# An attention-and-FFN kernel on one Trainium2 core: part of the sync engine's transfers re-ordered at the start of the FFN stage and at each change of token group

## The reference

```python
h  = einsum('bct,bcd->bdt', x, cond_weights[itok])       # a 64x64 mix per sequence
x  = x + attention(h)      # 16 heads of 32, 8 key/value heads, rope, the best 32 of 64 keys per head
hx = x @ W.T + scalings[a] * ((x @ A[a].T) @ Bm[a].T)    # a linear layer with a rank-16 adapter per sequence
Wg, Wu, Wd = dequant_nvfp4(...)                          # 4096x512, 4096x512, 512x4096, four-bit codes with scales
inter = gelu(hx @ Wg.T) * (hx @ Wu.T)
out   = x + inter @ Wd.T
```

## Time and profile before

| | before |
|---|---|
| median of 3 runs | 2748.27 us (2748.01 to 2749.01) |
| the profiled execution | 2745.64 us, of which the span from first to last instruction is 2744.1 us |
| PE busy | 2588.6 us, 94% of the span |
| PEld, DVE busy | 2171.9 us (79%), 1964.2 us (72%) |
| ACT, POOL busy | 881.2 us (32%), 977.2 us (36%) |
| mean granted TensorE clock | 0.984 of full |
| SP's queue of transfers | 481.17 MB, 48.1% of the 16 engines' time |
| from 753 to 1950 us | transfers busy 78%, 290 GB/s; POOL busy 623.88 us |
| from 1950 us to the end | transfers busy 53%, 198 GB/s; POOL busy 28.30 us |

### The profile page before, as it was taken

The page is one execution under the profiler, slowest core; times in us unless marked ns, Lnnn a source line. Parts: engine busy times, 40 slices in busy tenths (PEclk is TensorE's granted clock), DMA queues, the critical chain, the costliest instruction groups (busy, mean ns, idle before and its releaser), DMA issues.

```text
span 2744.1 us, 38773 instructions
## 1 busy us (share of the span) xinstructions
PE 2588.6 (94%) x13824; PEld 2171.9 (79%) x13824; DVE 1964.2 (72%) x3084; ACT 881.2 (32%) x1530; POOL 977.2 (36%) x1189
## 2 busy tenths in 40 slices
PE   5888999898889989999999999999999999999999
PEld 4777888787768778788887778887888888888887
DVE  6887777878569778788887788888854554545555
ACT  4445445454322222222222222222222222222222
POOL 3554434534246445555554455555410000000000
PEclk9999999999999999999999999999999999999999
DMA  3223222322679888758887866678645744664363
GB/s 119 84 94 105 81 96 93 105 87 86 242 293 326 334 314 319 280 216 327 306 325 279 329 246 240 223 288 306 237 167 216 272 154 165 226 261 158 146 250 138
DMA packets 173617, 585.34 MB, mean 213 GB/s; under 512 B 22136, under 2 KB 81400, under 8 KB 139008
## 3 DMA queue, kind: packets, MB, share of 16 engines
q1 hardware_dynamic: 138112, 481.17, 48.1%
q0 software_dynamic: 35328, 101.82, 10.0%
HBM read 446.14 MB, written 136.71 MB: 212 GB/s over the span
## 4 chain that ended last, share of the span: by engine, by line
PE 75%; DMA 11%; DVE 8%; issue 2%; ACT 2%; SPq 1%; POOL 0%; DVEq 0%; ACTq 0%; POOLq 0%
PE bank_a L866 22%; PE down L883 21%; PE proj L693 11%; PE bank_b L866 11%; DMA out<-acc 7%; PE bank_c L866 6%; DMA gu_slot<-w_scratch 4%; PE scores L733 1%; PE pv L758 1%; PE scores L742 1%; DVE probs L1259 1%; DVE hs L1193 1%; DVE rope_sin L1213 1%; DVE row_sum L1252 1%; DVE rope_in L1215 1%
## 5 line engine op out<-in xcount | busy, mean ns | idle before, releaser
L883 PE MATMUL down<-d_slot,inter_parts 128*128 128x512 f32 x3072 | 737.4, 389 | 0.0
L883 PEld LDWEIGHTS down<-d_slot,inter_parts 128*128 128x128 f32 x3072 | 576.6, 188 | 119.7
L1092 ACT ACTIVATE copy_p<-bank_a 128x512 f32<-128x512 f32 x384 | 229.7, 598 | 798.0 <-PE bank_a L866 798.0
L866 PE MATMUL bank_a<-h_ahead,gu_slot 128*128 128x512 f32 x1536 | 402.8, 399 | 46.8 <-DMA gu_slot<-w_scratch 43.4
L1401 DVE TENSOR_TENSOR acc<-down,acc 128x512 f32<-128x512 f32 x512 | 349.6, 686 | 88.4 <-PE down L883 60.7
L866 PE MATMUL bank_a<-h_once,gu_slot 128*128 128x512 f32 x1536 | 390.0, 389 | 1.4 <-ACT copy_p L1092 1.4
L866 PEld LDWEIGHTS bank_a<-h_ahead,gu_slot 128*128 128x128 f32 x1536 | 295.1, 193 | 113.3 <-DMA gu_slot<-w_scratch 47.6
L866 PEld LDWEIGHTS bank_a<-h_once,gu_slot 128*128 128x128 f32 x1536 | 288.2, 188 | 61.9 <-ACT copy_p L1092 2.2
L574 POOL TENSOR_TENSOR lut_v<-lut_v,signed_scale 128x512 f32<-128x512 f32 x96 | 124.4, 1296 | 495.0 <-DVE lut_v L1182 494.3
L1386 DVE TENSOR_TENSOR up<-gate,up 128x512 f32<-128x512 f32 x256 | 214.0, 836 | 87.7 <-ACT gate L1102 73.9
L1109 ACT ACTIVATE inter_parts<-up 128x512 fp32r<-128x512 f32 x256 | 159.4, 629 | 271.0 <-PE down L883 158.8
(11 more groups left out here) (123 smaller groups left out, 3536.1 us busy)
## 6 DMA issues: line engine op xcount, KB each, us to landing
gu_slot<-w_scratch SPq DMA_DIRECT2D x128, 1792.0 KB, 8.5
d_slot<-d_scratch SPq DMA_DIRECT2D x64, 1024.0 KB, 10.4
w_scratch<-w_parts POOLq DMA_DIRECT2D x96, 512.0 KB, 7.7
h_ahead<-h_scratch SPq DMA_DIRECT2D x44, 1024.0 KB, 11.7
h_once<-h_scratch SPq DMA_DIRECT2D x33, 1024.0 KB, 7.6
h_scratch<-h_out SPq DMA_DIRECT2D x32, 896.0 KB, 5.0
acc<-out SPq DMA_DIRECT2D x22, 1024.0 KB, 5.9
out<-acc SPq DMA_DIRECT2D x22, 1024.0 KB, 13.6
```

The costliest lines, as they stand in the source:

```text
L866: ins = pe.matmul(bank[:], gu_slot[n % 2][:, w, u, c * P:(c + 1) * P], mat(v, h)[:, c, part, :], start=(start and c == 0 and i == 0), stop ...
L883: ins = pe.matmul(bank[:], inter_parts[:, j, u, q, e * P:(e + 1) * P], d_slot[m % 2][:, j, part, :], start=(j == 0 and i == 0), stop=(j == ...
L1092: act.activation(copy[:], bank_a[n % 2][:], ACT.Copy).then_inc(copied, 1)
```

## The change

Only the order of issue changes; every transfer, product and addition of the kernel before is still there.

1. The second half of the last tile's hidden rows: `hidden_high(NT - 1, 1)` goes from unit 0 to unit 1 on ACT, `hidden_low(NT - 1, 1)` from unit 0 to unit 1 on DVE, and its store on SP from before the loop to the turn n = 1, behind `load_gate_up(2)`. SP's waits for all hidden rows and all x rows go to n = 2, behind `load_gate_up(3)`.
2. `turn_acc(m - 2, FIRST_HALF)` stands ahead of `load_down(m)` and of its wait.
3. The early token matrices of the next visit are loaded in the units `since` = 2 to 5 where the running visit has three blocks, and 3 to 6 where it has more, in place of 1 to 4.

```diff
             store_hidden(NT - 1, 0)
-            store_hidden(NT - 1, 1)
-            for q in h_stored:
-                sp.wait_ge(q, NT * 16)
-            sp.wait_ge(x1_stored, NT * 16 + PRIMED)
...
                     load_gate_up(n + 1)
+                if n == 1:
+                    store_hidden(NT - 1, 1)
+                if n == 2:
+                    for q in h_stored:
+                        sp.wait_ge(q, NT * 16)
+                    sp.wait_ge(x1_stored, NT * 16 + PRIMED)
+                if j == 1 and m >= 1 and LAST[m - 1]:
+                    turn_acc(m - 1, SECOND_HALF)
                 if j == 0:
+                    if m >= 2 and LAST[m - 2]:
+                        turn_acc(m - 2, FIRST_HALF)
                     if m >= 2:
                         sp.wait_ge(down_full, 8 * (m - 1))
                         passed()
                     load_down(m)
-                    if m >= 2 and LAST[m - 2]:
-                        turn_acc(m - 2, FIRST_HALF)
-                elif m >= 1 and LAST[m - 1]:
-                    turn_acc(m - 1, SECOND_HALF)
...
-                if v + 1 < NV and 1 <= since <= AHEAD_MATS:
-                    load_mat(v + 1, since - 1)
+                lead = since - (3 if len(VISITS[v][1]) > 3 else 2)
+                if v + 1 < NV and 0 <= lead < AHEAD_MATS:
+                    load_mat(v + 1, lead)
...
                 if n == 0:
                     hidden_high(NT - 1, 0)
+                elif n == 1:
+                    hidden_high(NT - 1, 1)
                 elif n % 2 == 0:
                     inter_high(n - 1, FIRST_HALF)
                 copy_product(n, p5_full, copy_p5, p5_copied, up_added[SECOND_HALF])
                 gelu_first(n)
                 gelu_second(n)
-                if n == 0:
-                    hidden_high(NT - 1, 1)
...
                 up_second(n)
+                if n == 1:
+                    hidden_low(NT - 1, 1)
                 add_down(m - 1, NE * j)
...
                 gelu_times_up(n, SECOND_HALF)
-                if n == 0:
-                    hidden_low(NT - 1, 1)
                 add_down(m - 1, NE * j + 2)
```

## The result

The changed kernel took 2685.57 us (median of 4 runs, 2684.07 to 2689.63) against 2748.64 us for the kernel before in the same comparison (4 runs, 2748.01 to 2751.52): a ratio of 0.9771, 95% interval 0.9754 to 0.9788, or 63 us less. The forecast was 2703.4 with a range of 2690 to 2722. The direction was right and so were the two places of the gain, the start and the changes of visit; the gain was 18 us larger than forecast, and the time lies 4.4 us under the range. The trace is of the execution that took 2689.63 us.

A forecast was written before the change was run, and what follows sets the result against it. PE was taken to bound the kernel, its FFN stage losing 69.9 us at the start and seven changes of visit. Savings of 35.2 and 9.7, together 44.9 us, from the median 2748.27 gave 2703.4 us, range 2690 to 2722.

The forecast's parts named there:

- the start: Units 0 to 2 of the FFN stage: moving the last tile's second-half rows saves 9.7 us (7 to 11).
- the size of the turns of the accumulator: Changes of visit: with two transfers fewer ahead of the blocking store, 35.2 of 55.2 us lost go.
- debit: Blocking store on SP: standing right behind gate and up costs it 0.8 us more (at most 1.65).
- the wait given for visit 6: PE's wait for gate and up weights at visit 6: 2.2 us left, plus 1.4 us of low clock.
- the dear bound: SP's queue: a transfer of 1024 KB costs at most 4.75 us, read from a store right behind gate and up.
- the extra matrix of the short visits: Visits 1 and 2: an early matrix ahead of the next weights costs 3.1 us, so they come only 2.3 sooner.
- the swap of a matrix for the down weights: Behind the store in long visits: down weights replace a same-sized matrix at no cost; weights come 5.4 us sooner.
- good end: Whole forecast: 4.75 us a transfer, no debit, 47.7 us gained at changes of visit and 11 at the start; 2689.
- rival (a): Start and changes of visit: all loss goes, the store gaining 9.5 us and the start 11; 2682 us, chance 0.06.
- (b): Blocking store: lands no sooner, waiting for its own write and POOL's stores; 3.5 us gained, 2745, chance 0.05.
- (c): Down weights behind the blocking store land too late for the first down chunk; slower, 2754 us, chance 0.03.
- The price by bytes alone: SP's queue: 1.05 MB cost 2.4 us, not 3.1; the store gains 4.0 us, total near 2710.

The follow-up runs named there:

- part 3 undone: Changed kernel with the early token matrices loaded in units 1 to 4 of a visit again; 2740.88 us.
- part 2 undone: Changed kernel with the down weights issued ahead of the blocking first-half accumulator store again; 2695.58 us.
- quiet kernel: Kernel before without the FFN stage's dequantisation on DVE and POOL, the first three blocks' weights serving all sixteen; 2692.13 us.
- one unit later still: Changed kernel with down weights one unit later at changes of visit, behind that unit's gate and up weights, and later early matrices in three-block visits; 2682.72 us.
- part 1 undone: Changed kernel with the last tile's second-half rows back in unit 0 and ahead of unit 2's weights on SP; 2696.35 us.
- part 3 alone: Kernel before with only the early token matrices loaded one or two units later; 2702.72 us.

## Why the prediction missed, point by point

**The mechanism and the start were right.** Part 1 was forecast at 9.7 us; the trace gives 14.7 - 5.0 = 9.7, and undoing it 8.5 in the FFN stage and 10.8 in the time. Its parts came out nearly as worked: unit 1's third product 0.64 us late (0.8 forecast), unit 2's first copy 1.37 us late (1.4 forecast), unit 2 at 779.43 - 757.08 = 22.4 us behind the first unit (22.6 forecast), and its own length 796.06 - 779.43 = 16.6 us (16.4 forecast). That the sum agrees to 0.1 us is luck, as two misses of 0.2 us cancel. No cover failed: PE never waited for down weights or a token matrix.

**The step that failed is the size of the turns of the accumulator**, "1024 KB more cost 3.3 and 3.1 us; I take 3.1", with its debit of 0.8 and the waits that it left: 13.0 us and 7.0 us of low clock behind them. Two waits of 2.9 us in sum and 2.6 us besides were left, 1.8 of these in the one unit with low clock; the wait given for visit 6 is gone too. Three terms were off, each by about 1 us or less and all the same way:

- The store was to land 5.4 us sooner; it landed 6.3 us sooner in the mean (15.1 after the store before, not 21.4), 7.3 at visit 1. The gaps between successive landings, as means over the seven changes, show where it came from. In the kernel before, the matrix took 3.0 us and the down weights 3.8, together 6.8, where 2 x 3.1 = 6.2 was put from the one row of visit 1. The moved store took 3.5 us behind gate and up, against 3.0 behind the down weights: a debit of 0.5, not 0.8; 6.8 - 0.5 is the 6.3. With one of the two put back the store came 3.3 us later (the matrix, part 3 undone, 18.4) and 3.7 us later (the down weights, part 2 undone). The 4.75 us of the earlier trace rows, from which the debit and the dear bound were taken, is one sample. The same gap, from gate and up to the first store of a turn, was 3.0 to 6.1 us over the seven changes before; the moved store's is 871.56 + 13.1 - (871.11 + 10.4) = 3.15 us at visit 1 in the changed kernel, and 3.1 to 4.6 over the seven; in the quiet kernel the first store's is 2.6 at visit 1 and at most 2.9. So most of what exceeds 2.6 us goes with POOL's work, and a store in that place has no fixed price.
- Behind the store, the extra matrix of the short visits (1 and 2, where the running visit has three blocks) was priced at 3.1 us; from the second store's landing to the next weights' it became 17.1 us at visit 1 (886.25 + 15.5 - 884.66, where 884.66 = 871.56 + 13.1) against 15.1 before, 2.0 more; at visit 2 it was 2.6 more.
- In long visits the swap of a matrix for the down weights was priced at nothing. There the stretch got 1.0 us shorter (14.4 against 15.4, mean of five).

So the weights came 5.3 and 4.6 us sooner in the short visits (2.3 forecast) and 6.9 in the long ones (5.4 forecast). A wait is the part of an arrival beyond a limit: with 4 to 8 us of lateness to remove at six of the seven changes, 1 to 3 us more of shift decided between a wait with low clock behind it and none. Five of the seven changes crossed that line entirely, and at visit 1 only 0.85 us stayed, with no fall of the clock. The miss of 14.5 us in the FFN stage (59.4 less 35.2 and 9.7) is this. The other 3.7 us to the 63.1 of the medians can't be placed: the medians are of more executions than the two traced ones.

**The range was the second fault.** Its good end, 2689, let the debit go and took 4.75 us a transfer, yet still left 4.7 us of waits, since it charged the short visits' matrix the same 4.75. One price was used for both sides of the store, so a high price helped in front and hurt behind. The two sides are separate quantities, and the case where both turn out well was left to rival (a) at 0.06. Its time, 2682, was nearest, though not by its condition (the store gained 6.3, not 9.5, and the start 9.7, not 11).

**The rivals.** (b), a store that waits for itself and for POOL: refuted, as it lands 6.3 us sooner with two transfers taken out. But POOL's share, named there, proved to be the other half of the cause. (c), late down weights: not seen, even one unit later still.

**The price by bytes alone.** By the Trainium skill (DMA: Bandwidth & Descriptors, "Anatomy of one DMA") the prediction reckoned 2.4 us for 1.05 MB, as an estimate, and a total near 2710. The Trainium skill gives this fit for transfers that GpSimd issues; those priced here are SP's. The runs went the other way from the forecast: 3.0 us for the matrix and 3.8 for the down weights ahead of the store, with POOL's transfers beside them. In the quiet kernel the matrix and the store behind the down weights took 2.6 us at the first change of visit, close to 2.4, and the down weights 3.2. The working has a slip: by this price the waits left come to 18.5 us, 5.5 more than 13.0 and not 6 to 7; with a whole fall of the clock behind visit 6 in place of a half it is 6.9 us, so that the total stands.

**Inside the change,** part 3 carries it. Alone it took the changes of visit from 55.2 to 9.2 us; part 2 added 5 to 7 us on top of it (9.2 to 4.3, 12.3 to 5.5) and nothing without it; part 1 is independent.

## What to carry to other kernels

Where one engine issues all transfers in order and waits for a store, list what stands between the last landing and that store, and between that store and the next load with a due time: a load whose use lies two units away belongs behind both, and moving it just across the store is worth little. Price the two stretches separately and beside the traffic of other queues, and from more than one sample, as the same transfer's gap differed by up to 3 us from visit to visit. A mean is not enough: with part 2 undone the loads came 0.9 us later in the mean, but 1.9 to 3.4 us later at three of seven changes, five loads were late, and it cost 7 us. When a forecast turns on arrivals within a few us of a limit, let the range hold the case that all of them make it.

## What the runs showed that was not expected

**The length of a wait alone did not tell whether the clock fell.** In the changed kernel PE waited 2.08 us at 993.92, began near full pace, and the clock fell some 1.3 us later (a mean of 0.82 over the 2.08 us of the first stretch, with 1.00 and 0.50 as the two levels); busy times and granted clock (the column behind POOL) of three stretches:

```profile
993.92:996.00 2.08, 2.08 (x8) 1.66 (x9) 0.00 (x0) 0.23 (x1) 0.00 (x0) 0.82 1.05 437
996.00:999.00 3.00, 3.00 (x9) 2.38 (x8) 0.67 (x2) 0.37 (x1) 0.00 (x0) 0.55 1.03 442
999.00:1003.00 4.00, 4.00 (x19) 3.25 (x19) 3.89 (x6) 1.42 (x3) 3.29 (x4) 1.00 0.98 411
```

In the kernel before, the clock did not fall behind a longer wait, 2.54 us at 992.58:

```profile
992.58:995.00 2.42, 2.42 (x10) 1.99 (x11) 0.00 (x0) 0.60 (x1) 0.00 (x0) 1.00 0.98 402
995.00:998.00 3.00, 3.00 (x15) 2.49 (x14) 2.24 (x3) 0.60 (x1) 0.96 (x1) 1.00 0.75 292
```

So the fall to 1.2 GHz cost 1.8 us behind the shorter wait (a unit of 16.74 us, not 14.96) and there was none behind the longer. Waits of 1.99, 2.10 and 2.16 us at the same visit, with part 1 undone, part 2 undone and part 3 alone, had no fall behind them either. What decides it stays open.

**The untouched token stage differs by up to 8.6 us.** The first FFN unit began between 748.64 us (part 2 undone) and 757.23 us (part 1 undone) in the nine traces; without the earliest of them they differ by 3.8 us. In the stretch from 50 to 100 us the mean granted clock differed too, 0.92 in the earliest and 0.77 to 0.90 in the others, but in no clear order: the second earliest, at 753.41, had 0.77. What sets the difference stays open. It is as large as what parts 1 and 2 are worth, so the FFN stage of the trace was the better measure for them.
